# Two indirect gathers under way at a time, in the sampling stage of a two-layer vision model

## What is computed

```python
def gather(yi, xi):
    idx = (yi * Ww + xi).reshape(N, -1)
    return jax.vmap(lambda im, ix: im[:, ix])(xf, idx)
v00 = gather(y0i, x0i); v01 = gather(y0i, x1i)
v10 = gather(y1i, x0i); v11 = gather(y1i, x1i)
out = v00 * (1 - wx) * (1 - wy) + v01 * wx * (1 - wy) + v10 * (1 - wx) * wy + v11 * wx * wy
```

## Time and profile before

| | |
|---|---|
| Median of 3 runs | 9661.08 us (9647.11 to 9673.49) |
| Profiled execution, its own time | 9657.97 us |
| Its span, first to last instruction | 9656.2 us |
| Mean granted TensorE clock | 0.894 of full speed |
| PE busy | 7727.8 us (80%) |
| DVE busy | 5175.6 us (54%) |
| POOL busy | 5070.2 us (53%), DMA issue by its own instruction counted |
| Gathers' queue (q0) | 639.57 MB, 21.2% of 16 DMA engines' span |
| Sampling's gathers | from 528.8 to 7124.8 us of the span |

### The profile page before, as it was taken

How to read it: one execution, slowest core, us unless ns; L and a number is a source line. 1 busy time by engine, 2 the same in 40 slices (tenths; PEclk the granted TensorE clock), 3 DMA queues, 4 the chain that set the end, 5 groups by cost and what they waited for, 6 DMA issues and landing times. The chain is left out here.

```text
span 9656.2 us, 96652 instructions
## 1 busy us (share of the span) xinstructions
PE 7727.8 (80%) x31522; PEld 4168.2 (43%) x31522; DVE 5175.6 (54%) x10029; ACT 3767.1 (39%) x5495; POOL 5070.2 (53%) x4864
## 2 busy tenths in 40 slices
PE   7637776645894799869999977997999799989699
PEld 3623333433442344434444433443444344435466
DVE  6543335545564566656666555665653466634233
ACT  2101102201462266525666533662666255541232
POOL 1057777667777777777777777777730000001322
PEclk9868888867897799988999988997999799999799
DMA  3844335666543544454444355445430311115221
GB/s 129 289 150 137 120 119 178 213 217 211 161 138 112 175 138 144 130 179 126 138 139 146 119 176 180 142 129 178 137 101 28 94 46 46 40 45 157 81 73 54
DMA packets 658546, 1283.59 MB, mean 133 GB/s; under 512 B 189043, under 2 KB 398218, under 8 KB 643408
## 3 DMA queue, kind: packets, MB, share of 16 engines
q0 software_dynamic: 234240, 639.57, 21.2%
q1 hardware_dynamic: 405392, 562.58, 19.5%
q10 hardware_dynamic: 18432, 75.51, 2.0%
HBM read 1003.44 MB, written 278.91 MB: 133 GB/s over the span
## 5 line engine op out<-in xcount | busy, mean ns | idle before, releaser
L727 POOL DMA_INDIRECT sa_slot<-s_table,sa_rec x4608 | 4812.6, 1044 | 2279.2 <-issue 1382.9
L1704 DVE CUSTOM_DVE_ANT_0 a_above<-a_late,a_above 128x512 f32<-128x512 f32 x1600 | 1101.6, 689 | 1436.5 <-PE a_late L1556 1321.5
L1636 ACT ACTIVATE a_p<-a_s 128x1024 f32<-128x1024 f32 x1600 | 1628.6, 1020 | 124.4 <-PE a_s L1594 122.6
L1611 PE MATMUL a_ctx<-a_p,a_v 128*64 128x512 f32 x6400 | 1577.3, 614 | 85.0 <-issue 84.5
L1645 ACT ACTIVATE a_above<-a_diff 128x512 f32<-128x512 f32 x1600 | 956.6, 598 | 1648.2 <-PE a_diff L1544 1379.7
L769 DVE TENSOR_TENSOR sa_slot<-sa_slot,sa_q 128x1152 f32<-128x1152 f32 x512 | 694.0, 1355 | 1021.6 <-DMA sa_slot<-s_table,sa_rec 1005.1
L1594 PE MATMUL a_s<-a_q,a_k 98*128 98x512 f32 x3200 | 1047.3, 411 | 3.2 <-ACT a_p L1636 3.2
L878 PE MATMUL sa_sums<-keep_ident,sa_vals 128*128 128x128 f32 x4608 | 681.3, 297 | 420.9 <-DVE sa_vals L821 420.9
L1556 PE MATMUL a_late<-a_k,a_q 96*128 96x512 f32 x1600 | 815.2, 510 | 168.0 <-DVE a_pair_max L1704 164.6
L1544 PE MATMUL a_diff<-a_kd,a_q 96*128 96x512 f32 x1600 | 725.5, 453 | 194.8 <-DMA a_q<-s_q 157.6
L878 PEld LDWEIGHTS sa_sums<-keep_ident,sa_vals 128*128 128x128 f32 x4608 | 609.5, 155 | 518.6 <-DVE sa_vals L821 439.4
(11 more groups left out here) (280 smaller groups left out, 8089.3 us busy)
## 6 DMA issues: line engine op xcount, KB each, us to landing
sa_slot<-s_table,sa_rec POOLq DMA_INDIRECT x4608, 3.1
s_table<-t_rows ACTq DMA_DIRECT2D x64, 1024.0 KB, 7.7
a_q<-s_q SPq DMA_DIRECT2D x480, 128.0 KB, 3.5
s_part<-a_o SPq DMA_DIRECT2D x160, 256.0 KB, 2.4
t_qwin<-s_dwq SPq DMA_DIRECT2D x64, 512.0 KB, 6.9
t_kvwin<-s_dwkv SPq DMA_DIRECT2D x64, 386.0 KB, 10.3
a_kd<-s_kd SPq DMA_DIRECT2D x384, 64.0 KB, 3.4
a_o<-s_part SPq DMA_DIRECT2D x96, 256.0 KB, 3.6
```

The source lines that it names most:

```text
L727: pool.indirect_dma_start(out=self.slot[g][:, k, :, :, :].rearrange("p c a n -> p (c a n)"), out_offset=None, in_=self.s["table"][n // TIL ...
L1611: mm = pe.matmul(self.ps_ctx[i * 2 * HD:(i + 1) * 2 * HD, :], self.v_and_ones(run.head, kb), self.p[slot % P_SLOTS][:, i * CHUNK:(i + 1) * ...
L1636: act.activation(self.p[slot % P_SLOTS][:, :], self.ps_s[slot % 2], ACT.Exp, scale=float(HD) ** -0.5).then_inc(self.exped, 1)
L1704: dve.tensor_tensor_reduce(above, self.ps_late, above, 1.0, LOWEST, ALU.add, ALU.max, self.pair_max[:, t, j:j + 1]).then_inc(self.late_got, 1)
```

## The change

At most two gathers are under way. Gather k of a group waits until gather k - 2 has landed; the first two of a group wait for the last two of the group before. A group's gathers increment two semaphores in turn ("lanes": points 0, 2, 4, 6, 8 and points 1, 3, 5, 7), in place of the first seven and the last two.

```diff
-EARLY = 7
+UNDER_WAY = 2
...
-        self.gathered = [r.sem(f"gathered{g}") for g in range(G)]
-        self.gathered_late = [r.sem(f"gathered_late{g}") for g in range(G)]
+        self.landed = [[r.sem(f"landed{g}_{lane}") for lane in range(UNDER_WAY)] for g in range(G)]
...
+    def in_lane(self, lane):
+        return len(range(lane, K, UNDER_WAY))
+
     def gather(self, pool, n, g):
         if g == 0:
             pool.wait_ge(self.tile_in[n % 2], 32 * (n // 2) + 32)
         if n > 0:
             pool.wait_ge(self.values_made, G * (n - 1) + g + 1)
-        if G * n + g > 0:
-            before = G * n + g - 1
-            pool.wait_ge(self.gathered[before % G], 16 * EARLY * (before // G + 1))
         for k in range(K):
+            if k >= UNDER_WAY:
+                lane = k % UNDER_WAY
+                pool.wait_ge(self.landed[g][lane], 16 * (self.in_lane(lane) * n + k // UNDER_WAY))
+            elif G * n + g > 0:
+                before = G * n + g - 1
+                lane = (K - UNDER_WAY + k) % UNDER_WAY
+                pool.wait_ge(self.landed[before % G][lane], 16 * self.in_lane(lane) * (before // G + 1))
             pool.indirect_dma_start(
                 out=self.slot[g][:, k, :, :, :].rearrange("p c a n -> p (c a n)"), out_offset=None,
                 in_=self.s["table"][n // TILES].rearrange("t p (g n) -> (t p g) n", g=G),
                 in_offset=bass.IndirectOffsetOnAxis(ap=self.rec[n % 2][:, g * K + k:g * K + k + 1].bitcast(U32), axis=0),
-            ).then_inc(self.gathered[g] if k < EARLY else self.gathered_late[g], 16)
+            ).then_inc(self.landed[g][k % UNDER_WAY], 16)
...
     def q_times_k(self, dve, t, n, g):
-        dve.wait_ge(self.gathered[g], 16 * EARLY * (n + 1))
-        dve.wait_ge(self.gathered_late[g], 16 * (K - EARLY) * (n + 1))
+        for lane in range(UNDER_WAY):
+            dve.wait_ge(self.landed[g][lane], 16 * self.in_lane(lane) * (n + 1))
```

## The result

The changed kernel takes 11924.6 us (median of 4 runs, 11914.25 to 11932.82) against 9667.28 us for the kernel before beside it: a ratio of 1.234, 95% interval 1.232 to 1.236. The loss is 2257 us. The forecast was 11,600 us with a range of 10,900 to 12,400: the way and the mechanism as forecast, the size 320 us short.

What follows compares the result with a forecast made beforehand. POOL's gathers were taken to bound the kernel. (3.35 landing + 0.30 release)/2 x 4608 = 8410 us, plus 125 for group starts, gives 8535 against 6597: +1938 on 9658, so 11,600 us; range 10,900 to 12,400.

Steps and rivals of the forecast that it cites:

- POOL sets the pace: From first gather to last, POOL's issue bounds the flow; each added microsecond, 1938 in all, passes to the end.
- rival (c): Gather landings shorten with two under way: at 2.4 us, 1.35 us a gather, 9,280 us in all; chance 0.02.
- Release: Time from a landing to the waiting gather's start on POOL: 0.30 us for eight of nine, 0.79 for the ninth.
- Rival (a): Every gather's release on POOL costs 0.79 us, so 2.07 us a gather, 12,600 us in all; chance 0.12.
- The sum: POOL's gathers: half of landing plus release, 1.825 us, times 4608, plus 125 us for group starts: 8535 us.
- The landing term: Time from a gather's start to its landing: 3.35 us, the middle between median 3.1 and estimated mean 3.6.
- rival (b): TensorE's granted clock falls to 0.59 as it pauses more, adding 340 us in attention: 11,900 us; chance 0.09.
- The rule of the Trainium skill: A gather's transfer takes 2.3 us, so 1.3 us a gather with two under way and no loss at all.

Runs made afterwards that it cites:

- depth1: The changed kernel with one gather under way in place of two; 19135.97 us (one run).
- depth3: The changed kernel with three gathers under way, three semaphores a group in turn; 9987.2 us, ratio 1.035 to the kernel before.
- early5: The kernel before, with a group's first gather waiting for the first five of the group before, not seven; 9483.9 us, ratio 0.983.
- early2: The kernel before, with a group's first gather waiting for the first two of the group before, not seven; 9448.02 us, ratio 0.979.
- two_waits: The changed kernel, each gather from k = 1 on also waiting for the tile's long-met record, ahead of its landing's wait; 12623.88 us (one run).
- swap_after: The changed kernel with a group's first gather waiting first for the landing, then for the slot (values_made); 11783.65 us.
- depth4: The changed kernel with four gathers under way; 9650.49 us, ratio 0.9994 to the kernel before.

## Why the prediction was right, and where it was short

*POOL sets the pace*: right. In the changed kernel, depth1 and depth3 the time moved as the stretch of the gathers did, +2257 for +2271, +9485 for +9478, +336 for +334 us. Downwards it follows less closely: -167 for -194 us in early5, -202 for -226 in early2.

*Landing, rival (c), that it shortens enough to pay*: rejected, and rightly. The minimum was 2.8 us before and 2.7 with four, three, two and one under way, and the median went from 3.1 with four to 3.0 and, with one, 2.9. The rival needed 2.56. The quiet landing did not come down, but with other work beside it the mean did. For the 384 gathers whose landings the trace before has, it was 3.74 us; the same 384 have 3.34 with two under way and 3.03 with one. With the sampling alone the mean over all 4608 is 3.03 us by the old rule and 3.07 with two. So the direction of this rival was real in the whole kernel, and its size far from paying.

*Release*: I took 0.30 us for eight gathers and 0.79 for the ninth; the bare release is 0.26 and 0.76. The step that I had from the earlier trace rows and the code, that a second wait is what makes a release long, is shown by two_waits and by swap_after. Rival (a) put the long release on every gather and came to 12,600 us; two_waits, which does this to the kernel, took 12,624. That the two agree so closely is in part luck, since (a) used the same sum, and what this sum gets wrong is next.

*The sum*: 1.825 us and 125 us for the starts, 1.852 a gather together, against 1.924 measured: 8867 - 8535 = 332 us short, and the time was short by about as much. The step that fell short is "two gathers pass in one landing plus one release". It needs the two chains to be independent, and they share POOL: when a landing comes while POOL is busy with the other chain's gather, the gather behind it starts only 0.30 us after that one has ended. Of the 4030 pairs of landing and start that the changed kernel's trace has, 969 are such, and they start 0.69 us after the landing in the mean. Over all pairs the start comes 0.425 us after the landing. The sum had 0.354 (0.30 and a ninth of 0.49), which is 0.071/2 x 4608 = 164 us too little. The bare release alone would be 0.316: the hindrance is 251 us, and my release, too large by 88 us, hid a part of it. The mean landing of 3.385 us in place of 3.35 adds 81 us. The other 87 us lie in group 5, whose landings the trace lacks: its gathers took 2.06 us each, the others 1.905.

*The landing term*: 3.35 us against a measured mean of 3.385 is luck in part. It was the middle of two bounds, and no row said where between them the truth would lie. The lower, 3.1 us, and the prediction's "no landing under 2.8 us in 4608" are of the 384 gathers that the earlier trace rows counts. The upper, 3.6 us, is not the mean that it is called: it adds the average of excesses, none of which can be negative, to 2.96, which makes it too high, and takes a gather at 1.25 us where the mean is 1.044 + 0.305 = 1.35, which makes it too low. The mean of the 384 was 3.74, outside both bounds; the term came out near the mark because landings shortened with two under way, which the sum did not have.

*TensorE's clock, rival (b)*: the granted clock fell to 0.78 over the flow as this rival expects, but the time behind the gathers' stretch grew by 10 us and VectorE held POOL back for 8.6 us in all. No price of it is to be seen.

The rule of the Trainium skill ("DMA: Bandwidth & Descriptors", section "Anatomy of one DMA — SWDGE (gpsimd) path"), 2.0 us and the bytes, was put at 2.3 us as an estimate for these 131,072 bytes. In the timeline of depth1 the landing comes 2.9 us after the start of an instruction of 0.95 us, so 1.95 us after its end: the rule is 0.35 us over if it is counted from the end of the issue, and 0.6 us short if it is read as the whole. Read as the whole it would have forecast no loss.

## What to carry to other kernels

Before putting a limit on transfers under way, work out (landing + release)/limit and compare it with the issue time: here 2.9 + 0.26 against 1.25 us, so two are too few, three nearly enough and four free. With quiet numbers this is a floor and not the time: it gives 1.58 us for two and no loss for three, and 1.924 and 336 us were measured. Find the engine whose waits on all others are near nothing; a microsecond added there is a microsecond of the kernel, and a wait removed there is a cheap gain until another engine sets the pace (EARLY = 2: 2.1%). Where an instruction has two waits, put first in the program the one that will end last.

## What the runs showed of the hardware

A GpSimd indirect DMA with one wait starts 0.26 us after the landing that meets it; with two, where the landing is the second in the program, 0.76 us. Adding a second wait that had long been met to eight of nine gathers, ahead of the landing's, cost 699 us over 4096 gathers. One wait each, where it was met, cost nothing that could be measured (depth4).

With the sampling alone, a gather of 128 rows of 1,024 bytes landed 2.01 us after the end of its instruction in the mean, both by the old rule (3.03/1.326 = 2.3 under way on average) and with at most two. The instruction took 0.945 us with no VectorE instruction beside it, and 1.465 us in the mean beside line 775.

TensorE's mean granted clock over the flow went down as the gathers held its work up: 0.88 of full speed at a busy share of 77% before, 0.78 at 61% after. TensorE's busy time for the same matmuls rose from 5106 to 5426 us.
